# Four more down tiles in split form, other warm-up matmuls, and a new order of the first fifteen steps in a two-layer conditional residual kernel

## What is computed

```python
h = relu(x @ W1[id0] + b1[id0])                 # 512 -> 128
t = x + h @ W2[id0] + b2[id0]                   # 128 -> 512
x1 = x + layernorm(t) * gamma[id0] + beta[id0]
out = x1 + x1 @ W[id1] + b[id1]                 # 512 -> 512
```

## Time and profile before

| | |
|---|---|
| median of 3 runs | 312.26 us (312.13 to 312.66) |
| the profiled execution's own time | 311.37 us |
| its span in the trace | 309.6 us |
| PE busy | 302.4 us, 98% of the span |
| POOL, DVE, ACT busy | 71%, 73%, 68% |
| granted clock, whole span | 1.0 |

### The profile page before, as it was taken

The page is one execution under the profiler, slowest core; times in us unless marked ns, Lnnn a source line. Parts: engine busy times, 40 slices in busy tenths (PEclk is TensorE's granted clock), DMA queues, the critical chain, the costliest instruction groups (busy, mean ns, idle before and its releaser), DMA issues.

```text
span 309.6 us, 4831 instructions
## 1 busy us (share of the span) xinstructions
PE 302.4 (98%) x1424; PEld 244.1 (79%) x1424; DVE 224.8 (73%) x641; ACT 211.0 (68%) x381; POOL 220.9 (71%) x181
## 2 busy tenths in 40 slices
PE   7989999999999999999999999999999999999995
PEld 7535778788888888888888888888888888888884
DVE  0277999596968879596887969688795977889610
ACT  1149695957896859687596958968596874857431
POOL 0048999499699995999869995999959995631000
PEclk9999999999999999999999999999999999999999
DMA  6969968589976896868857897668867381111122
GB/s 215 346 245 323 318 236 269 163 254 285 271 164 198 252 296 182 234 198 233 264 187 202 227 325 223 137 196 266 286 189 207 125 284 36 68 69 71 68 102 102
DMA packets 40399, 64.34 MB, mean 208 GB/s; under 512 B 6068, under 2 KB 10164, under 8 KB 40372
## 3 DMA queue, kind: packets, MB, share of 16 engines
q1 hardware_dynamic: 38976, 61.41, 64.1%
q10 hardware_dynamic: 1396, 2.62, 2.5%
HBM read 47.24 MB, written 16.78 MB: 207 GB/s over the span
## 4 chain that ended last, share of the span: by engine, by line
PE 91%; DMA 4%; ACT 2%; DVE 1%; issue 1%; SPq 1%; ACTq 0%
PE out_ps L897 54%; PE h_ps L897 15%; PE down_ps L897 13%; PE turn_ps L965 9%; DMA xT<-x_cols 2%; DMA w<-w_all 2%; ACT y L411 1%; SPq L193 1%; DVE turn_ps L605 0%; DVE x1T_lo L612 0%; ACT out_sb L429 0%; ACT hT L393 0%; DVE y L561 0%; ACT w_hi L382 0%; PE out_ps L965 0%
## 5 line engine op out<-in xcount | busy, mean ns | idle before, releaser
L897 PE MATMUL out_ps<-x1T_hi,w_hi 128*128 128x512 f32 x256 | 100.6, 393 | 0.4 <-ACT out_sb L429 0.4
L897 PE MATMUL out_ps<-x1T_lo,w_hi 128*128 128x512 f32 x256 | 99.8, 390 | 0.0
L897 PE MATMUL out_ps<-x1T_hi,w_lo 128*128 128x512 f32 x256 | 99.7, 389 | 0.0
L798 POOL TENSOR_TENSOR xrow<-xrow,b_rows 128x512 f32<-128x512 f32 x60 | 77.3, 1297 | 3.7 <-DMA xrow<-x_rows 3.7
L420 ACT ACTIVATE x1T_hi<-turn_ps,gamma_beta 128x512 fp32r<-128x512 f32 x63 | 42.6, 689 | 40.7 <-DVE turn_ps L605 40.6
L803 POOL TENSOR_TENSOR xT_lo<-xT,xT_hi 128x512 fp32r<-128x512 f32 x48 | 62.1, 1295 | 5.8 <-ACT xT_hi L363 5.8
L605 DVE SCALAR_TENSOR_TENSOR turn_ps<-turn_ps,gamma_beta,xT 128x512 f32<-128x512 f32 x63 | 44.8, 752 | 28.5 <-PE turn_ps L965 27.7
L411 ACT ACTIVATE y<-y,shift,rstd 128x512 f32<-128x512 f32 x64 | 51.4, 816 | 19.3 <-DVE shift L596 18.7
L897 PEld LDWEIGHTS out_ps<-x1T_hi,w_hi 128*128 128x128 f32 x256 | 48.1, 188 | 10.8 <-ACT out_sb L429 0.7
L897 PEld LDWEIGHTS out_ps<-x1T_lo,w_hi 128*128 128x128 f32 x256 | 48.1, 188 | 10.1
L897 PEld LDWEIGHTS out_ps<-x1T_hi,w_lo 128*128 128x128 f32 x256 | 48.1, 188 | 10.0 <-issue 0.2
(11 more groups left out here) (53 smaller groups left out, 362.5 us busy)
## 6 DMA issues: line engine op xcount, KB each, us to landing
out_cols<-out_sb SPq DMA_DIRECT2D x64, 256.0 KB, 2.7
xrow<-x_rows SPq DMA_DIRECT2D x29, 512.0 KB, 6.4
xT<-x_cols SPq DMA_DIRECT2D x28, 512.0 KB, 6.3
w<-w_all SPq DMA_DIRECT2D x8, 1024.0 KB, 7.0
w<-w_all SPq DMA_DIRECT2D x15, 256.0 KB, 4.4
b_rows<-b_all SPq DMA_DIRECT2D x8, 256.0 KB, 7.5
xT<-x_cols ACTq DMA_DIRECT2D x4, 256.0 KB, 3.9
xT<-x_cols ACTq DMA_DIRECT2D x2, 512.0 KB, 6.7
```

Source lines behind the costliest of these rows:

```text
L798: nc.gpsimd.tensor_tensor(xrow[:, i % XR, :], xrow[:, i % XR, :], b2_rows[:, m % 2, :], ALU.add).then_inc(rowbias_done, 1)
L897: mm = nc.tensor.matmul(out, lhsT, rhs, start=first and n == 0, stop=last and n == len(terms) - 1, skip_group_check=unchecked)
```

## The change

1. `PLAIN_DOWN` goes from 8 to 4 tiles. Tiles 4 to 7 of `down` (block 1) are split, so W2 of sample 0 and h of block 1 now need a high and a low part: `w2_high(0)`, `h_high(1)` on ACT, `w2_low(0)`, `h_low(1)` on POOL.
2. The warm-ups multiply a tile `busy` that DVE fills, instead of the identity; six run first, three after `seed(0)` and one after `seed(1)`, which now stands ahead of `up(0)`.
3. ACT issues all its loads first: tiles 0, 1, 2 of `xT`, rows 4 and 5 (512 KB), the ids, tile 3, tiles 4 and 5, tiles 6 and 7. `load_table` moves behind `w_high(0, 2)`.
4. SP's list is in another order: `load_b1(0)` and `load_w2(0)` ahead of b2, `load_rows(6)` next, `load_w(0)` behind tiles 8 to 11 of `xT`.
5. The hand-written lists of the five engines for the first 15 steps are in another order. The steps from 15 on are unchanged.

```diff
-    PLAIN_UP, PLAIN_DOWN = 4 * BLOCK, 2 * BLOCK
+    PLAIN_UP, PLAIN_DOWN = 4 * BLOCK, 1 * BLOCK
...
+            nc.vector.memset(busy[:], 1.0).then_inc(busy_done, 1)
             nc.vector.memset(eps[:], EPS).then_inc(eps_done, 1)
...
             def warm_up(n):
                 for _ in range(n):
-                    nc.tensor.matmul(turn_ps[0][:, :P], ident[:], ident[:], start=True, stop=True)
+                    nc.tensor.matmul(turn_ps[0][:, :P], busy[:], busy[:], start=True, stop=True)
...
                 wait_cols(pe, k)
+                if k == 0:
+                    pe.wait_ge(ident_done, 1)
...
-            pe.wait_ge(ident_done, 1)
-            warm_up(12)
+            pe.wait_ge(busy_done, 1)
+            warm_up(6)
             opening()
```

More of the change, by code:

```diff
@@ L106, in cond_resid_kernel @@
         eps = sb("eps", [P, 1])
+        busy = sb("busy", [P, P])
         table = sb("table", [P, 1])
@@ L498, in opening @@
                 normalise(11)
+                w_high(1, 1)
+                w_high(1, 2)
                 w_high(1, 3)
-                h_high(4)
                 standard(12)
+                standard(13)
                 finish(4)
-                finish(5)
                 x_hi(20)
                 x1_high(8)
-                x_hi(21)
[L507 to L512, removed]
+                x1_high(9)
+                finish(5)
+                relu(4)
+                h_high(4)
+                finish(6)
+                x1_high(10)
+                standard(14)
+                x1_high(11)
+                x_hi(21)
                 normalise(12)
@@ L618, in opening @@
                 add_bias(0)
+                add_bias(1)
+                add_bias(2)
                 statistics(0)
+                add_bias(3)
+                statistics(1)
                 mean_variance(0)
[L621 to L625, removed]
                 rstd_start(0)
@@ L738, in opening @@
                 rstd_end(13)
+                mean_shift(12)
+                mean_variance(14)
                 x1_low(10)
                 x1_low(11)
-                mean_shift(12)
                 mean_shift(13)
@@ L833, in opening @@
             def opening():
+                w2_low(0)
+                bias_rows(4)
+                bias_rows(5)
+                bias_rows(6)
+                bias_rows(7)
+                h_low(1)
                 w_diagonal(0)
                 w_low(0, 0)
-                bias_rows(4)
-                bias_rows(5)
                 w_low(0, 1)
@@ L859, in opening @@
                 bias_rows(15)
+                w_low(1, 0)
+                w_low(1, 1)
+                w2_low(2)
+                x_lo(20)
                 bias_rows(16)
-                w_low(1, 0)
-                x_lo(20)
-                w_low(1, 1)
+                bias_rows(17)
                 w_low(1, 2)
+                h_low(4)
                 w_low(1, 3)
-                bias_rows(17)
-                h_low(4)
-                w2_low(2)
             def step(s):
@@ L992, in opening @@
                 seed(0)
+                warm_up(3)
+                seed(1)
+                warm_up(1)
                 up(0)
```

283 lines of the change are left out of this document (141 added, 142 removed).

## The result

The changed kernel takes 311.51 us (median of 17 runs, 311.02 to 312.93), the kernel before beside it 312.41. The ratio is 0.9969, with a 95% interval of 0.9955 to 0.9983: 0.9 us faster, clear of noise, where 2.0 us were forecast. The profiled execution has 311.31 us and a span of 309.5 us, next to 311.37 and 309.6 before. The execution profiled before was 1 us faster than its median, this one lies 0.2 under its own, so the two traces hardly differ in length although the medians do: the last pair of turns before 100 us starts at 98.09 in the trace before and at 98.11 here.

What follows compares the result with a forecast made beforehand. PE was taken as the bound, busy 302.4 of 309.6 us. Terms 0.72 + 1.5 + 0.44 + 0.6 - 1.25 gave 2.0 us saved, so 312.26 - 2.0 = 310.3 us, range 309.0 to 312.0.

Steps and rivals of the forecast that it cites:

- 2: Hole ahead of up(6): xT tiles 6 and 7 issued earlier close it, W1 staying just in time; gain 1.5 us.
- 3: seed(1) ahead of up(0): its transposes lie in PE's wait for W1; gain 0.44 us.
- 4: Warm-ups before the first up: PE's clock is up by 7.67 us, cost 0, bounds 0 and 3.4 us.
- loads in the order of issue: Rival: W1 quarters stand behind 0.75 MB more of ACT's loads, costing 1.8 us (312.1) or half (311.2); chance 0.20.
- Terms 1: Four down tiles split instead of plain: 0.72 us less PE work.
- 6: Hole before out(6): closes because out(6) needs only finish(4); gain 0.6 us, or 0.
- Term 5: New PE waits: 0.25 us at down(4), 0.8 at turn(0), 0.2 at out_part(0, 1); sum 1.25 us, bounds 0 and 2.5.
- the chain keeps up: Rival: normalise starts 0.8 us earlier ahead of turn(0), giving 309.4 us or a little below; chance 0.12.
- Term 7: Parts without effect: two table loads, the first hidden even 0.8 us late; load_w(0) landing later but in time.

Runs made afterwards that it cites:

- e3_rows_last: Changed kernel with rows 4 and 5 moved from fourth to last of ACT's opening loads: 312.10 us, ratio 0.9976 to the kernel before.
- e7_gate_first: Changed kernel, but ACT waits for the first W1 quarter before issuing rows 4 and 5, then xT tiles 6 and 7: 309.56 us, ratio 0.9914.
- e12_gate_again: Same kernel as e7_gate_first, run again beside the changed kernel: 310.01 us, ratio 0.9927 to the kernel before.
- e5_plain8: Changed kernel with eight plain down tiles again, without the split of tiles 4 to 7 and its casts: 312.08 us, ratio 0.9973.
- e10_before_gate: Kernel before, with xT tiles 6 and 7 issued once the first W1 quarter is in, ahead of relu(0): 311.32 us, ratio 0.9957.
- e8_gate_hlow_first: e1_gate with one more edit, POOL doing h_low(1) ahead of bias_rows(4) to (7): 314.09 us, ratio 1.0051 to the kernel before.
- e1_gate: Changed kernel, but ACT issues xT tiles 6 and 7 and rows 4 and 5 only after the last W1 quarter landed: 315.73 us, ratio 1.0103.
- e6_warm12: Changed kernel with twelve warm-ups together ahead of seed(0), none between the seeds: 311.58 us, ratio 0.9961 to the kernel before.
- e4_before_loads_first: Kernel before with only ACT's loads in the new order, all ahead of relu(0): 313.41 us, ratio 1.0030.
- e2_late: Changed kernel with xT tiles 6 and 7 and rows 4 and 5 issued behind relu(0), without a wait: 317.01 us, ratio 1.0142 to the kernel before.

## Why the prediction was wrong

- **The failed step** is in 2, and 3 and 4 lean on it: "W1's last quarter ... comes perhaps 0.6 us later than 9.3 ... and is due at 10.3". It was used at 12.61, and 13.37 in the second trace: the step put the cost of sharing at nothing, and the runs show 2.26 us at the mark. I had seen the rule (packet by packet) and carried over the wrong number: at 7 to 8 us SP's queue moved 0.07 MB, but at 4 to 7 us 0.04 to 0.05 per us, which was the rate of W1, and with ACT's queue busy past 12 us instead of to 8.1 all of W1 had to pass at such a rate (0.20 MB in the 4 us from 6 to 10), not only its last 0.05 MB. Besides, SP's queue began a microsecond later. A smaller slip: the quarter issued at 3.9 with 5.4 us to landing is the third; the last was issued at 4.5 and took 5.0, so 9.5 and not 9.3. The rival "loads in the order of issue" had the place, and nearly the price (1.8 us for 2.3), at a chance of 0.20; its rule is not what the runs bear out: in `e3_rows_last` the rows are issued behind W1's first quarters, and W1 was no earlier. Its range of 311.2 to 312.1 holds the result.
- **The range** held the result (309.0 to 312.0), the sign was right, the size was not: 0.9 for 2.0 us. With W1 nearer its time, in `e7_gate_first`, the gain is 2.7 us by the ratio (2.3 in `e12_gate_again`) and 1.9 us of span.
- **Terms 1, 2, 6**: the hole before `up(6)` and that before `out(6)` closed as worked out. The split's term is in keeping with `e5_plain8`, no more, and half of it seems to be lost in the wait at `turn(0)`. In `e10_before_gate` the second hole is closed too, without the new order of the lists, which I had put down to that order.
- **Term 3** held: `seed(1)` lies in the wait for W1, and only two seeds are left behind the mark.
- **Term 4** was right: no clock loss. The six records from 5.88 take 0.11 us each, so the clock had risen by then, with four transposes amid the warm-ups. The same list rose at about 4.5 us in `e8_gate_hlow_first` and at 7.0 in `e1_gate`. Had the transposes not counted for the clock, as I read the Trainium skill (TensorE: Matmul & The Clock Gate, Part 4), the clock would have risen in the first `up`; no run shows that.
- **Term 5** was too high by a third, and its rival "the chain keeps up" half right. From start to start in `e7_gate_first`: `down(4)` is 0.4 us late (16.89 + 6 x 0.86 = 22.05, starts 22.47; 0.25 forecast), `turn(0)` 0.45 (24.82 to 25.27; 0.8 forecast), `out_part(0, 1)` not at all (0.2 forecast). The four `normalise` took 2.93 us, not 3.17. In the changed kernel itself `down(4)` is 0.34 us late (18.94 + 6 x 0.86 = 24.10, starts 24.44) and `turn(0)` 0.45 (26.80 to 27.25). The margins at `turn(4)`, `up(16)` and `turn(8)` held.
- **Term 7** held only because W1 was late too: b1 was in at 13.37 instead of 10.2, and `relu(0)` behind the table load ended at 15.35, when `down(0)` was due (15.28). In `e6_warm12` the same costs 0.4 us.
- **The sum again**, with the measured stalls of the changed kernel: 0.72 + 1.5 + 0.44 + 0.6 less 0.79 is 2.5 us, and less 2.26 for the mark 0.2 us, next to 0.1 us between the two spans. That the medians are 0.9 us apart and not 0.1 would fit an early W1 in the one execution profiled before, but there is only one trace of that kernel, so why the medians differ more than the traces stays open.
- The late start of SP's queue goes with the rows issued at 2.12, ahead of SP's first load at 2.8, and not with the amount: all five traces that have them there (the changed kernel twice, `e4_before_loads_first`, `e5_plain8`, `e6_warm12`) show no packet of SP before 5 us, and the nine others 34 to 102 packets at 4:5. By what means is open.
- Left open too: how `e7_gate_first` would fare with its wait at another quarter.

## What to carry to other kernels

A load that is issued earlier takes its share from what is already waited for: before loads are moved to the front, name the smallest transfer that PE waits for and ask what will be outstanding beside it, above all if its packets are smaller than the others'. A wait for the first piece of the urgent transfer, ahead of the bulk, was worth 1.4 to 1.9 us here, more than the whole reordering. And a row that an in-order engine needs for side work (here POOL's bias) can stand in front of what the main path needs; moving its load has to be followed through that engine's list.

## What the runs showed of the hardware

- While both queues had work (the changed kernel, 6 to 10 us), the one with 512-byte rows (W1) moved 0.02 to 0.08 MB per us and the other 0.19 to 0.23; the numbers of packets were close, 440 and 453 in all, though not in each us (180 to 110 at 6:7, 94 to 108 at 7:8, 56 to 116 at 9:10). The Trainium skill (DMA: Bandwidth & Descriptors, Queues, rings and completion order) says that each engine takes turns between the queues packet by packet; the counts over 4 us agree, the megabytes show what it means for small packets.
- Four 64 KB loads took 5.1 to 8.8 us each to land with 2.5 MB ahead or beside them (the changed kernel twice and `e3_rows_last`), and with 1.5 MB 4.7 to 5.4 us in the kernel before and 3.7 to 4.7 us in `e10_before_gate`.
- Behind a hole of 4.5 us PE ran at half its clock for some 3.5 us in `e1_gate` (27.16 to about 30.8) and some 4.5 us in `e2_late` (28.8 to about 33.3). Behind the hole of 2.8 us in the trace of `e8_gate_hlow_first` it kept its clock (1.00 in all stretches from 28 to 36 us). Of the twelve executions of that kernel, though, six have a mean granted clock of 0.993 to 0.995, and they are 0.7 us longer in the mean; only one was traced.
